# Running ScalarE's rounding ahead of its sign floors in a spiking FFN kernel, with one multiply moved to ScalarE and three weight loads held back

## The reference

```python
rates = jax.nn.relu(inputs) * DT
c = initial_state[:, None, :] + jnp.cumsum(rates, axis=1)
fl = jnp.floor(c)
prev = jnp.concatenate([jnp.floor(initial_state)[:, None, :], fl[:, :-1, :]], axis=1)
spikes = (fl - prev) / DT
...
logits = x_flat @ router_w.T
probs = jax.nn.softmax(logits, axis=-1)
top_v, top_i = jax.lax.top_k(probs, K)          # K = 2, capacity C per expert
...
h = jax.nn.gelu(jnp.einsum('ech,ehf->ecf', expert_in, w1), approximate=False)
y = jnp.einsum('ecf,efh->ech', h, w2)
out = out + tok * (gate * keep)[:, None]
return x + out
```

## Time and profile before

| | us |
|---|---|
| median of 3 runs | 66.87 (66.67 to 68.95) |
| the profiled execution, its own time | 67.07 |
| its span, first to last instruction | 65.3 |
| PE busy | 53.2 |
| DVE busy | 36.0 |
| ACT busy | 27.2 |
| POOL busy | 20.3 |

### The profile page before, as it was taken

The page is one execution under the profiler, slowest core; times in us unless marked ns, Lnnn a source line. Parts: engine busy times, 40 slices in busy tenths (PEclk is TensorE's granted clock), DMA queues, the critical chain, the costliest instruction groups (busy, mean ns, idle before and its releaser), DMA issues.

```text
span 65.3 us, 1164 instructions
## 1 busy us (share of the span) xinstructions
PE 53.2 (82%) x374; PEld 30.7 (47%) x374; DVE 36.0 (55%) x158; ACT 27.2 (42%) x45; POOL 20.3 (31%) x60
## 2 busy tenths in 40 slices
PE   3997899999655897999939999999999999992000
PEld 1322354535321261434348669976696656570000
DVE  3498796695368786799989706593150022035000
ACT  0599836739242249629994301870054020000000
POOL 6799984400001056008887600000000000002820
PEclk9999999999999555555799999999999999999965
DMA  0499999999999999800587844998999950000210
GB/s 0 107 379 292 364 328 357 353 350 343 336 349 348 348 348 349 255 21 0 153 246 234 293 180 81 291 304 239 354 385 386 388 168 0 0 0 0 82 60 10
DMA packets 13545, 14.82 MB, mean 227 GB/s; under 512 B 648, under 2 KB 13040, under 8 KB 13536
## 3 DMA queue, kind: packets, MB, share of 16 engines
q1 hardware_dynamic: 12608, 12.62, 60.2%
q0 software_dynamic: 816, 2.01, 9.6%
q10 hardware_dynamic: 112, 0.07, 0.5%
HBM read 13.08 MB, written 2.36 MB: 237 GB/s over the span
## 4 chain that ended last, share of the span: by engine, by line
PE 47%; DVE 14%; ACT 10%; issue 9%; DMA 6%; POOL 6%; ACTq 2%; DVEq 0%; POOLq 0%
PE bank L702 22%; PE bank L686 12%; DMA w_got<-in_L_ffn_w_dram,w_index 6%; DVE x_lo L936 4%; ACT x_hi L805 4%; PE bank L546 3%; POOL out_dram L520 3%; ACT w_got L793 3%; PE bank L718 2%; ACT L793 2%; PE bank L551 2%; POOL lead_cum L492 2%; DVE ev_lane L1029 1%; ACTq L789 1%; DVE floors L950 1%
## 5 line engine op out<-in xcount | busy, mean ns | idle before, releaser
L532 PE MATMUL bank<-ones_b 128*128 128x512 bf16 x35 | 14.2, 536 | 1.1 <-POOL ones_b L419 1.1
L702 PE MATMUL bank<-w_sb,spare_sb 128*64 128x256 f32 x128 | 14.7, 382 | 0.0
L702 PEld LDWEIGHTS bank<-w_sb,spare_sb 128*64 128x64 f32 x128 | 8.8, 137 | 4.5
L520 POOL DMA_INDIRECT out_dram<-floors,out_index x2 | 2.0, 1019 | 23.3 <-DVE floors L1139 23.0
L686 PE MATMUL bank<-ev_pair,w_got 128*128 128x128 f32 x64 | 7.8, 278 | 1.1 <-DMA w_got<-in_L_ffn_w_dram,w_index 1.1
L686 PEld LDWEIGHTS bank<-ev_pair,w_got 128*128 128x128 f32 x64 | 7.4, 192 | 1.6 <-DMA w_got<-in_L_ffn_w_dram,w_index 1.6
L839 ACT ACTIVATE spare_sb<-bank 128x512 f32<-128x512 f32 x8 | 4.8, 597 | 6.4 <-PE bank L686 6.0
L1046 DVE TENSOR_SCALAR rate<-bank,pair_gate 128x256 f32<-128x256 f32 x4 | 1.9, 485 | 9.5 <-PE bank L702 9.5
L936 DVE SCALAR_TENSOR_TENSOR x_lo<-x_sb,x_hi 128x512 fp32r<-128x512 f32 x8 | 5.6, 701 | 2.7 <-ACT x_hi L805 2.7
L501 POOL DMA_INDIRECT w_got<-in_L_ffn_w_dram,w_index x4 | 4.1, 1024 | 4.8 <-issue 4.8
L532 PEld LDWEIGHTS bank<-ones_b 128*128 128x128 bf16 x35 | 3.3, 114 | 4.5 <-issue 2.9
(11 more groups left out here) (217 smaller groups left out, 79.5 us busy)
## 6 DMA issues: line engine op xcount, KB each, us to landing
w_sb<-in_L_ffn_w_dram SPq DMA_DIRECT2D x8, 1024.0 KB, 11.2
x_sb<-in_x_dram SPq DMA_DIRECT2D x8, 256.0 KB, 4.8
out_dram<-x_sb SPq DMA_DIRECT2D x1, 2048.0 KB, 13.9
cond<-in_cond_dram ACTq DMA_DIRECT2D x2, 32.0 KB, 2.1
w_got<-in_L_ffn_w_dram,w_index POOLq DMA_INDIRECT x4
cond<-in_cond_dram SPq DMA_DIRECT2D x1, 32.0 KB, 1.9
x_rows<-in_x_dram,out_index POOLq DMA_INDIRECT x2
out_dram<-floors,out_index POOLq DMA_INDIRECT x2, 3.1
```

Source lines behind the costliest of these rows:

```text
L520: g.indirect_dma_start(out=out_rows[:, :], out_offset=bass.IndirectOffsetOnAxis(ap=out_index[:, t:t + 1], axis=0), in_=ffn_out[:, t, :], i ...
L532: nc.tensor.matmul(bank[2][:, 0:4 * P], ones_b[:, :], ones_b[:, :].unsqueeze(1).to_broadcast([P, 4, P]), start=True, stop=True)
L702: mm = nc.tensor.matmul(Y[d % 2][at, :], hT[:, d % 2, f, at], w2_sb[:, 2 * d + side, f, :], start=(f == 0), stop=(f == FC - 1))
```

## The change

Five edits. (1) In the front loop ScalarE rounds two groups between sign floors in another order: groups 2 and 3 before the floor of group 1, 4 and 5 before that of 3, 6 and 7 before those of 5 and 6. Its copy for `theta3` stands behind two roundings instead of one, and its second clearing of `w1_got` moves from the front of the loop to a place after the lists. VectorE's order is written out to go with it. (2) Two more warming products stand ahead of the loop, seven for five. (3) `lead_ones` is made by ScalarE instead of GpSimd. (4) `make_index(0)` stands ahead of `make_lanes(2)`. (5) Three w2 loads wait for the gathers, not two.

```diff
@@ block.sync
-                if e == E - 2:
+                if e == E - 3:
                     for d in range(D):
                         sp.wait_ge(w1_in[d], 16)
@@ block.gpsimd
-            g.tensor_scalar(lead_ones[:, :], ones_b[:, :], lead[:, 0:1], None, ALU.mult).then_inc(lead_mats, 1)
@@ block.tensor
-            keep_warm(5)
+            keep_warm(7)
...
-            pe.wait_ge(lead_mats, ST + 1)
+            pe.wait_ge(lead_mats, ST)
+            pe.wait_ge(lead_ones_set, 1)
@@ block.scalar
-            clear_got(1)
...
             take_rates(0)
+            take_rates(1)
             act.wait_ge(theta_rest, 1)
             nc.scalar.copy(theta3[B:2 * B, :], theta_r[B:2 * B, :]).then_inc(theta_set, 1)
-            take_rates(1)
             act.wait_ge(masks, 6)
-            for g in range(2, XG):
-                take_rates(g)
-                if g - 1 in SIGN_GROUPS:
-                    sign_floors(g - 1)
+            take_rates(2)
+            take_rates(3)
+            sign_floors(1)
+            take_rates(4)
+            take_rates(5)
+            sign_floors(3)
+            take_rates(6)
+            take_rates(7)
+            sign_floors(5)
+            sign_floors(6)
...
+            clear_got(1)
...
+            act.wait_ge(lead_set, 1)
+            nc.scalar.activation(lead_ones[:, :], ones_b[:, :], ACT.Copy, scale=lead[:, 0:1]).then_inc(lead_ones_set, 1)
             act.wait_ge(turned_s, ST)
@@ block.vector
-            dve.wait_ge(theta_rest, 1)
-            v.tensor_tensor(theta3[2 * B:, :], theta_r[2 * B:, :], theta_mid[2 * B:, :], ALU.subtract).then_inc(theta_set, 1)
...
             take_rests(0)
+            dve.wait_ge(theta_rest, 1)
+            v.tensor_tensor(theta3[2 * B:, :], theta_r[2 * B:, :], theta_mid[2 * B:, :], ALU.subtract).then_inc(theta_set, 1)
             take_rests(1)
...
+            take_floors(0)
+            take_rests(2)
+            take_rests(3)
+            take_floors(2)
+            take_rests(4)
...
+            take_floors(7)
...
             make_lanes(1)
+            make_index(0)
             make_lanes(2)
-            make_index(0)
```

More of the change, by code:

```diff
@@ L280, in adaln_ffn_kernel @@
         lead_mats = sem("lead_mats")
+        lead_ones_set = sem("lead_ones_set")
         lead_counts = sem("lead_counts")
@@ L939, in take_rests, with take_floors @@
                                        ALU.max, ALU.subtract).then_inc(rests, 1)
+            def take_floors(g):
+                dve.wait_ge(cums, g + 1)
+                if g >= RING:
+                    dve.wait_ge(weighed, g - RING + 1)
+                v.tensor_scalar(floors[:, g % RING, :, :].rearrange("p j c -> p (j c)"), CUM[g % 4][:, 0:GW],
+                                0.0, -0.5, ALU.is_ge, ALU.add).then_inc(floored, 1)
             take_rests(0)
+            dve.wait_ge(theta_rest, 1)
+            v.tensor_tensor(theta3[2 * B:, :], theta_r[2 * B:, :], theta_mid[2 * B:, :], ALU.subtract).then_inc(theta_set, 1)
             take_rests(1)
@@ L944, in _ @@
             v.tensor_copy(routerT[:, :, :], bank[5][:, 0:KC * E].rearrange("p (k e) -> p k e", k=KC)).then_inc(router_out, 1)
-            for g in range(XG):
-                if g not in SIGN_GROUPS:
-                    dve.wait_ge(cums, g + 1)
-                    if g >= RING:
-                        dve.wait_ge(weighed, g - RING + 1)
-                    v.tensor_scalar(floors[:, g % RING, :, :].rearrange("p j c -> p (j c)"), CUM[g % 4][:, 0:GW],
-                                    0.0, -0.5, ALU.is_ge, ALU.add).then_inc(floored, 1)
-                if g + 2 < XG:
-                    take_rests(g + 2)
-                dve.wait_ge(vec, steps[0])
-                if g == 0:
-                    dve.wait_ge(router_out, 1)
-                    loose(v.tensor_scalar(router_s[:, :, :], routerT[:, :, :], SPIKE, None, ALU.mult))
-                if g == 1:
-                    loose(v.tensor_copy(router3[:, 0, :, :], router_s[:, :, :]))
-                if g == 2:
-                    loose(v.tensor_tensor(router_r[:, :, :], router_s[:, :, :], router3[:, 0, :, :], ALU.subtract))
-                if g == 3:
-                    loose(v.tensor_copy(router3[:, 1, :, :], router_r[:, :, :]))
-                if g == 4:
-                    v.tensor_tensor(router3[:, 2, :, :], router_r[:, :, :], router3[:, 1, :, :], ALU.subtract).then_inc(router3_set, 1)
+            take_floors(0)
[3 more added lines that the diff above has]
+            take_rests(4)
+            dve.wait_ge(router_out, 1)
+            loose(v.tensor_scalar(router_s[:, :, :], routerT[:, :, :], SPIKE, None, ALU.mult))
+            take_rests(5)
+            dve.wait_ge(vec, steps[0])
+            loose(v.tensor_copy(router3[:, 0, :, :], router_s[:, :, :]))
+            take_floors(4)
+            dve.wait_ge(vec, steps[0])
+            loose(v.tensor_tensor(router_r[:, :, :], router_s[:, :, :], router3[:, 0, :, :], ALU.subtract))
+            take_rests(6)
+            dve.wait_ge(vec, steps[0])
+            loose(v.tensor_copy(router3[:, 1, :, :], router_r[:, :, :]))
+            take_rests(7)
+            dve.wait_ge(vec, steps[0])
+            v.tensor_tensor(router3[:, 2, :, :], router_r[:, :, :], router3[:, 1, :, :], ALU.subtract).then_inc(router3_set, 1)
+            take_floors(7)
             dve.wait_ge(weighed, XG)
```

## The result

The changed kernel takes 64.41 us (median of 4 runs, 63.9 to 64.53) against 67.12 us for the kernel before on the same chip. The ratio is 0.960, with a 95% interval of 0.951 to 0.970. The forecast was 64.8, with 64.0 to 66.0 as its range. The profiled execution took 64.45 with a span of 62.7, so the two profiled spans differ by 65.3 - 62.7 = 2.6 us. In what follows I account for these 2.6; they are the distance of one profiled execution from one other.

The account below looks back on a forecast made before the run. A latency chain across TensorE, ScalarE and VectorE bounds the front loop, 2.76 us a turn, no engine full. Terms 0.4, 1.6, 0.1 and zeros sum to 2.1 us: 67.07 becomes 64.97, less 0.2 gives 64.8, range 64.0 to 66.0.

Parts of the forecast that it names:

- Start of the loop: Ahead of the front loop: without ScalarE's clearing the first group comes earlier, gain 0.4 us, ends 0.2 and 0.6.
- A turn: Front loop, two groups of x: 2.73 us becomes 2.20, ends 1.95 and 2.55; three turns gain 1.6.
- rival (a): Front loop: VectorE becomes the bound at its upper cost, turn 2.5, gain 1.1, 65.8 us; chance 0.15.
- (d): Front loop: another wait replaces that behind the sign floor, turn above 2.55, 66.0 to 66.5 us; chance 0.08.
- (e): Front loop: the engines overlap better than the hand-overs assumed, turn 1.95, 64.0 us; chance 0.10.
- Behind the last product: End of the front loop: the last group's own latency stays, as its last floor waits for its bank.
- `lead_ones`: Router stage: moved off GpSimd, `kept` comes 0.1 us earlier since `limit_c` ends last; ends 0 and 0.2.
- `make_index(0)`: Behind the map products: gain 0 to 0.05; later ScalarE check just covered, taken as 0, loss up to 0.2.
- Held loads: w2 loads: third held load keeps the queue empty for the earlier first gather; cost 0, with 0.5 as end.
- The clock: Ahead of the product stage: nothing changes if TensorE's clock fall and rise move with the program, 0 us.
- (b): The second rival: TensorE's clock rise stays at 31.75, product stage loses 0.13 us, 64.9; chance 0.15.
- (c): Product stage: the clock rise is missed, first `hidden` and `project` at half rate lose 3 us, 67.7; chance 0.05.

Follow-up runs that it names:

- Experiment 9: The changed kernel with ScalarE's second clearing of `w1_got` back in front of the loop: 64.81 us, ratio 0.949.
- experiment 1: The kernel before with only the new ScalarE and VectorE orders in the front loop and the later second clearing: 65.91 us, ratio 0.968.
- experiment 7: The changed kernel with `lead_ones` back on GpSimd: 64.85 us, ratio 0.945.
- experiment 6: The changed kernel with `make_index(0)` back behind `make_lanes(2)`: 65.49 us, ratio 0.949.
- experiment 12: The changed kernel with VectorE's subtraction `shifted` moved earlier, right behind `make_index(0)`: 64.94 us, ratio 0.951.
- experiment 5: The changed kernel with two held w2 loads instead of three: 64.96 us, ratio 0.946.
- experiment 2: The changed kernel with the old ScalarE and VectorE orders in the front loop and the second clearing in front: 67.13 us, ratio 0.981.
- experiment 3: The changed kernel with VectorE's old order in the front loop, ScalarE's new one kept: 64.40 us, ratio 0.946.
- experiment 4: The changed kernel measured again without an edit: 64.65 us, ratio 0.944.
- experiment 8: The changed kernel with eight more tiny copies on ScalarE in its pause ahead of the lists: 64.67 us, ratio 0.944.
- experiment 10: The changed kernel with five warming products ahead of the loop instead of seven: 64.18 us, ratio 0.936.
- experiment 11: The changed kernel with GpSimd's gathers of x rows held until the first pair's two GELUs are done: 64.06 us, ratio 0.939.

## Why the prediction was right

**Start of the loop, 0.4.** Measured 0.43. Experiment 9 shows that the clearing was the cause (0.53 come back with it). The sequence of `theta_mid` and rest held as forecast, the first rest ran from 5.85 to 6.54. Two details were otherwise. The first rest product, at 6.67, starts 0.13 behind the rest, so TensorE was the later one here, by less than a tenth; what releases group 0 is the last part of `theta3`, which ends at 7.00, with the threshold products at 7.05 (7.49 before). The forecast had given it up to 0.1. And it took 0.215 us for each warming product; in three profiles the seven took 2.06 to 2.56 us instead of 1.68, and then the start was 0.2 to 0.7 late (8.25, 8.47 and 8.74 for 8.04).

**A turn, 2.20.** Measured 2.12, and experiment 1 gives the same with the loop alone. The gain of three turns is 1.82 instead of 1.6. TensorE's row of 2.10 for two groups was the right guide, as PE is busy through the first two turns. VectorE turned out nearly as tight (2.06 of the second turn's 2.12): three operations and the router ones almost fill it, so the 1.95 that I gave it by the spacing of 0.60 was too low, and rival (a)'s engine is close to a bound, at the forecast's own price. (The upper end is added up wrongly, too: 3 x 0.75 + 0.27 is 2.52, not 2.55.) Rivals (a), (d) and (e) have fallen by their numbers.

**Behind the last product.** I had let the last group's latency stay; it shrank by 0.28. All of it lies between the last `x_lo` product and the last floor (17.60 - 16.65 = 0.95 before, 15.07 - 14.40 = 0.67 now), and it is there with the loop alone (experiment 1); why is not shown. This term was missing.

**`lead_ones`, 0.1.** At `kept` it was 0.08, for the reason given: `limit_c` ends last. (The operation took 0.40 us on ScalarE, a little more than the 0.37 that was set as its bound, and fitted into the idleness.) But the same edit earned another 0.39 at the first gather (experiment 7). What failed in this term is that it counted only the rank product behind GpSimd's multiply: of a step taken away from a queue, what follows on the queue counts too.

**`make_index(0)`, 0.** Right: in experiment 6 the step to the gather is the same. The feared 0.2 through ScalarE's check is 0.12 at the first GELU, by experiment 12, which takes it away; it doesn't reach the end, as the second GELU stays.

**Held loads, 0, "guards the gain".** Right at the far end: the last projection doesn't wait. The last load lands at 48.7, earlier than the 49.3 to 50.2 that the forecast gives when moved by its own 2.1, and the copy lands 3.5 early. What the edit guards is not shown. It was not the first gather, as I thought, since that is not late with two held (experiment 5), and the longer stage there (25.25) stands beside stages as long with three held (experiments 2, 6 and 7). In time experiment 5 can't be told from the changed kernel, so this edit may be worth nothing.

**The clock, 0.** The product stage ran at 2.4 GHz from its start, so rivals (b) and (c) did not come true. In the profiled executions of experiments 1, 3 to 5 and 7 to 12 the rise lay between 27.7 and 30.0, ahead of the first product each time, in that of experiment 6 at 30.6, with 0.5 us to spare. It is not tied to the program, though. With the last weighing products at 15.8 in the changed kernel and 15.7 in its second profile, the clock fell at 18.5 in one and at 20.9 in the other, and rose at 28.7 and 27.8. The Trainium skill ("TensorE: Matmul & The Clock Gate", Part 1, What's actually happening) says that the monitor runs freely. The scatter of fall and rise in two profiles of one kernel agrees with that. But the second rival, a rise that stays near 31.75, did not come, because it took one draw for a fixed point. One chance was booked wrongly: rival (c)'s 67.7 is 1.2% above 66.87, so its 0.05 belonged to a change within 2% and not to a slower kernel.

**The sum.** Forecast 2.1, measured 2.60 between the profiles. Missing were 0.39 (queue of GpSimd), 0.28 (last group) and 0.22 (turn); too much by 0.28 (product stage) and 0.12 (gather to product). The terms that were worked out, start and turn, held in mechanism and size. That the time came within 0.4 us is in part luck, as 0.89 that were missing met 0.40 that were not foreseen. And the sum holds for the pair of profiles of the result only. In experiments 1 to 4 the whole change earns 3.4 us (68.03 to 64.65), of which the other four edits have 1.3, where the forecast gave them 0.1. That part of the prediction was too low. On top of the loop the 1.3 are 0.4 at the first gather and about 1.0 of a pause between the GELUs that is long with the loop alone and short in the changed kernel; for the pause no term stood in the sum.

## What to carry to other kernels

Where several engines hand a tile round and none is full, count the chain of one turn and what it covers; one more tile in hand lowers the turn only down to the busiest engine's work, here from 2.73 to 2.12. When an operation moves from one queue to another, look at every later operation of the old queue, not only at those who wait for its result. And a transfer that is needed late, such as the rows of x here, may disturb an engine that has nothing to do with it if it starts in a tight place. Warming products ahead of a loop can end up as the first term of its chain: look at how long they take in more than one execution.

## What the runs showed of the hardware

The first indirect gather on GpSimd started 3.91 to 3.92 us behind GpSimd's previous operation when its index was there in time (before, experiments 1 and 7), and 0.88 us behind the end of the index otherwise. It is no exact lower bound: in experiments 4 and 5 the gather that went by its index started 3.88 behind that operation. Nothing that the profile names lies in those 3.9 us.

With its input complete, ScalarE stood still for 1.28 us in the changed kernel (32.80, where the 2.05 of `hidden` end, to 34.08) and for 2.34 in experiment 1 (33.18 to 35.52), while two indirect gathers of x rows started; holding the gathers takes the pause away (experiment 11). I had not expected one to touch the other.

A 128x128 bf16 multiply by a column takes 0.60 us on GpSimd and 0.40 on ScalarE. Moved to the latter it was nearly free.

Seven equal warming products on TensorE, 128x512 in bf16 with nothing to wait for that the profile shows, took 1.68 us in five profiles and 1.72 to 2.56 in six others, at a granted clock of 1.00 in each.
